# The re-layout transfers of the kept exponentials move from SyncE's to ScalarE's queue, and the TensorE's background items get new steps

## The reference, cut to what matters

```python
q = _qz_ring(heads + rx_theta)                     # 16 heads of width 8, 4096 tokens an image here
scores = jnp.einsum('bhsd,bhtd->bhst', q, q) / np.sqrt(D)
attn = jax.nn.softmax(scores, axis=-1)
ctx = jnp.einsum('bhst,bhtd->bhsd', attn, q)
```

## Time and profile before

| | us |
|---|---|
| time before, median of 3 runs | 7771.48 (7758.5 to 7775.35) |
| the profiled execution, span | 7878.3 |
| ScalarE busy in it | 6811.0 (86%) |
| TensorE busy in it | 6921.9 (88%) |
| VectorE busy in it | 4954.8 (63%) |
| first and last exponential of the main stage | about 791 and 7635 |

### The profile page before, as it was taken

One profiled execution on the slowest core, in us unless ns is written; L12 is line 12 of the kernel. 1 busy time (PEld: TensorE's weight loads), 2 busy tenths in 40 slices (PEclk: granted clock), 3 DMA queues, 4 the chain that ended last, 5 costly groups with the idle time before them and its releaser, 6 DMA issues. The chain is left out here.

```text
span 7878.3 us, 154169 instructions
## 1 busy us (share of the span) xinstructions
PE 6921.9 (88%) x58691; PEld 1859.1 (24%) x58691; DVE 4954.8 (63%) x12688; ACT 6811.0 (86%) x5455; POOL 1244.3 (16%) x1165
## 2 busy tenths in 40 slices
PE   4555799999999999999999999999999999999987
PEld 1444121111121222222221212222222212222224
DVE  5566555555555777777676767777775545454763
ACT  1222799999999999999999999999999999999971
POOL 1553111111111112111221111121210000000000
PEclk8777899999999999999999999999999999999997
DMA  6776575757566556656564545554643333232338
GB/s 214 208 210 185 125 167 138 171 137 166 141 159 147 147 135 169 154 131 157 124 144 112 138 115 132 120 136 113 145 117 77 98 74 92 69 98 64 99 98 265
DMA packets 1744564, 1080.93 MB, mean 137 GB/s; under 512 B 347914, under 2 KB 1645632, under 8 KB 1742828
## 3 DMA queue, kind: packets, MB, share of 16 engines
q1 hardware_dynamic: 1650972, 767.00, 40.2%
q0 software_dynamic: 92880, 304.42, 13.9%
HBM read 410.43 MB, written 190.83 MB: 76 GB/s over the span
## 5 line engine op out<-in xcount | busy, mean ns | idle before, releaser
L1255 ACT ACTIVATE e<-sc 128x1536 f32<-128x1536 f32 x4192 | 5715.2, 1604 | 193.2 <-PE sc L1157 121.7
L1189 PE MATMUL acc<-e,v_cur 128*9 128x512 f32 x25152 | 3341.7, 599 | 45.5 <-DVE acc_sb L1092 44.4
L1157 PE MATMUL sc<-b_unit,a_cur 32*128 32x512 f16 x14592 | 1916.7, 388 | 358.3 <-ACT e L1255 277.2
L1157 PEld LDWEIGHTS sc<-b_unit,a_cur 32*128 32x128 f16 x14592 | 472.6, 91 | 3826.3 <-ACT e L1255 2890.3
L1151 DVE STREAM_TRANSPOSE e_turned<-e_turned 128x1024 f32<-128x1024 f32 x896 | 1060.7, 1221 | 147.9 <-DMA e_turned<-e_kept 114.8
L1255 ACT ACTIVATE e_kept<-sc 128x1536 f32<-128x1536 f32 x672 | 960.6, 1567 | 63.0 <-PE sc L1157 32.1
L757 POOL DMA_INDIRECT room<-taps,idx_st x432 | 520.4, 1205 | 2109.0 <-ACT e L1255 890.2
L757 POOL DMA_INDIRECT corners<-taps,idx_st x441 | 435.1, 987 | 2052.3 <-ACT e L1255 1563.5
L1189 PE MATMUL acc<-e_kept,v_cur 128*9 128x512 f32 x4032 | 715.0, 611 | 0.0
L1189 PEld LDWEIGHTS acc<-e,v_cur 128*9 128x9 f32 x25152 | 394.3, 88 | 797.9 <-issue 730.8
L1180 PE MATMUL acc<-e_turned,v_cur 128*9 128x256 f32 x7168 | 472.2, 381 | 0.0
(11 more groups left out here) (421 smaller groups left out, 5222.5 us busy)
## 6 DMA issues: line engine op xcount, KB each, us to landing
e_turned<-e_kept SPq DMA_DIRECT2D x3584, 128.0 KB
taps<-conv_vals SPq DMA_DIRECT2D x256, 288.0 KB
taps<-cf_tapped SPq DMA_DIRECT2D x128, 288.0 KB
ew<-in_ew SPq DMA_DIRECT2D x12, 1024.0 KB, 7.8
ew<-in_ew SPq DMA_DIRECT2D x48, 256.0 KB, 6.8
x_ch<-in_x SPq DMA_DIRECT2D x4, 2048.0 KB, 12.6
qn<-q SPq DMA_DIRECT2D x64, 128.0 KB
ctx<-ctx_t SPq DMA_DIRECT2D x128, 64.0 KB
```

The costliest lines, as they stand in the source:

```text
L1157: last = self.nc.tensor.matmul(self.sc[k % self.SC][:, i, :], self.a[rows, t * P:(t + 1) * P], self.bst[u % 2][rows, :], start=True, stop= ...
L1189: last = self.nc.tensor.matmul(self.acc[32 * h:32 * h + self.E1, :], self.v[:, t, h, :], src, start=(i == 0), stop=(i == self.UNIT - 1))
L1255: self.nc.scalar.activation(out, self.sc[k % self.SC][:], ACT.Exp, scale=1.0 / HD ** 0.5).then_inc(self.exp_done, 1)
```

## The change

Three things. First, the source layout: `e_kept` was indexed slab, then column; now it is column block (4), slab (9), 128 columns, so that what one transfer takes from a partition is one piece of 4 KB and not 8 pieces of 512 bytes. The exponential writes it in a pattern of 3 x 4 x 128, and the scores are read in the same order. Second, the 16 transfers of a half are issued by ScalarE, two behind each of eight exponentials, from the one that follows the third kept one. The waits of L1134 and L1136 stand in ScalarE's queue ahead of the first two. SyncE's queue loses them all. Third, `PLACES` has new steps for all kinds but "last"; order and number of the items are the same.

```diff
-    SHUFFLES = 16
+    SHUFFLES, ISSUES = 16, 8
...
-        self.kept = sb("e_kept", [P, 9, CHUNK])
+        self.kept = sb("e_kept", [P, 9 * CHUNK])
+        self.kept_by = self.kept[:].rearrange("p (c s x) -> p s c x", c=4, s=9)
...
-    def shuffle_sp(self, sp, qd, u, half):
...
-                sp.dma_start(dst.rearrange("p (s x) -> p s x", x=P), src).then_inc(self.shuffled[half], 16)
+    def shuffle_act(self, act, qd, u, half, part):
+
+
+        if part == 0:
+            used = self.plan.last_turned(u, half) + 1 if u else self.plan.last_turned(UNITS - 1, half) + 1 - UNITS * self.UNIT
+            act.wait_ge(self.pv_done, qd * (UNITS * self.UNIT) + (self.PV_START + used))
+            act.sem_inc(self.r.passed, 1)
+            act.wait_ge(self.exp_done, qd * self.QUAD_STEPS + (self.plan.halves[u, half] + 3 + self.SC))
+        for at in range(part * self.SHUFFLES // self.ISSUES, (part + 1) * self.SHUFFLES // self.ISSUES):
+            a, c = divmod(at, 4)
+            src = self.kept[32 * a:32 * a + 32, c * 9 * P:c * 9 * P + self.KEPT * P]
+            act.dma_start(self.turned[32 * c:32 * c + 32, a, half, :], src).then_inc(self.shuffled[half], 16)
...
-                    src = self.kept[:, self.WIDE * plan.kept_step[k][2] + at, :]
+                    src = self.kept_by[:, self.WIDE * plan.kept_step[k][2] + at]
...
+        issues = {k0 + 3 + i: (u, half, i) for (u, half), k0 in plan.halves.items() for i in range(self.ISSUES)}
...
-            self.nc.scalar.activation(out, self.sc[k % self.SC][:], ACT.Exp,
-                                      scale=1.0 / HD ** 0.5).then_inc(self.exp_done, 1)
+            self.nc.scalar.activation(out, src, ACT.Exp, scale=1.0 / HD ** 0.5).then_inc(self.exp_done, 1)
+            if k in issues:
+                self.shuffle_act(act, qd, *issues[k])
...
         "conv ffn": (
-            5, 25, 28, 46, 49, 51, 53, 55, 66, 72, 77, 78, 82, 85, 106, 109, 121, 124, 128, 129, 132, 144, 149, 154, 155, 156, 159,
+            5, 24, 26, 46, 48, 51, 53, 55, 65, 71, 74, 76, 77, 84, 106, 108, 121, 123, 126, 128, 130, 140, 146, 149, 151, 152,
...
-                    at.shuffle_sp(sp, qd, 0, 0)
...
-                at.shuffle_sp(sp, qd, 2 * p, 1)
```

More of the change, by code:

```diff
@@ L1251, in quad_act @@
                     act.wait_ge(self.shuffled[1 - half], qd * (self.BLOCKS * 16 * self.SHUFFLES) + (16 + 16 * self.SHUFFLES * blocks))
-                out = self.kept[:, self.WIDE * i:self.WIDE * (i + 1), :]
+                out, src = self.kept_by[:, self.WIDE * i:self.WIDE * (i + 1)], self.sc[k % self.SC][:].rearrange("p s (c x) -> p s c x", c=4)
             else:
-                out = self.e[plan.slot[k]][:]
-            self.nc.scalar.activation(out, self.sc[k % self.SC][:], ACT.Exp,
-                                      scale=1.0 / HD ** 0.5).then_inc(self.exp_done, 1)
+                out, src = self.e[plan.slot[k]][:], self.sc[k % self.SC][:]
+            self.nc.scalar.activation(out, src, ACT.Exp, scale=1.0 / HD ** 0.5).then_inc(self.exp_done, 1)
+            if k in issues:
+                self.shuffle_act(act, qd, *issues[k])
 def within(*buffers):
@@ L1604, in stage_main @@
         "conv first": (
[L1605 to L1606 removed]
+            2, 5, 7, 10, 12, 30, 31, 46, 48, 51, 53, 55, 62, 64, 69, 74, 88, 90, 94, 96, 98, 106, 110, 121, 125, 130, 158, 160,
+            164, 166, 168, 170, 172, 175, 178, 181, 195, 199, 204, 233, 235, 239, 241, 243, 245, 247, 250, 252, 256, 270, 294,
+            296,
         ),
         "conv": (
[L1609 to L1610 removed]
+            3, 5, 7, 9, 11, 19, 23, 46, 50, 55, 83, 85, 89, 91, 93, 101, 105, 121, 125, 130, 158, 160, 164, 166, 168, 170, 172,
+            175, 178, 181, 195, 199, 204, 233, 235, 239, 241, 243, 245, 247, 250, 252, 256, 270, 294, 296,
         ),
         "conv ffn taps": (
[3 rows of a table removed]
[4 rows of a table added]
         ),
         "conv ffn": (
[L1618 to L1620 removed]
+            5, 24, 26, 46, 48, 51, 53, 55, 65, 71, 74, 76, 77, 84, 106, 108, 121, 123, 126, 128, 130, 140, 146, 149, 151, 152,
+            159, 181, 183, 195, 198, 200, 202, 204, 215, 221, 223, 226, 227, 234, 256, 258, 260, 270, 272, 293, 295, 297, 299,
+            301, 303, 304,
         ),
         "ffn six": (
[3 rows of a table removed]
[3 rows of a table added]
         ),
         "ffn choice": (
[3 rows of a table removed]
[3 rows of a table added]
         ),
         "ffn": (
[3 rows of a table removed]
[3 rows of a table added]
         ),
         "last": (
[4 rows of a table removed]
[4 rows of a table added]
         ),
@@ L1701, in conv_quad @@
                     at.store_ctx(sp, qd, 2 * p - 1)
-                if not (first and p == 0):
-                    at.shuffle_sp(sp, qd, 2 * p, 0)
                 conv.load_sp(sp, n + LEAD + 1)
@@ L1728, in conv_quad @@
                 if p < QPAIRS - 1:
-                    at.shuffle_sp(sp, qd, 2 * p + 1, 0)
                     if first and p == 0:
@@ L1772, in last_quad @@
             store_gate(FFN_PAIRS)
-            for half in range(2):
-                at.shuffle_sp(sp, qd, 0, half)
             for u in range(1, UNITS):
```

9 lines of the change are left out of this document (removed), and 33 rows, old and new, of the table PLACES.

## The result

The changed kernel takes 8095.8 us, median of 4 runs (8090.4 to 8114.3), against 7772.9 (7758.5 to 7775.4): a ratio of 1.0424, 95% interval 1.0408 to 1.0440. That is 323 us slower where 40 us faster was forecast, and outside the range.

The account below looks back on a forecast made before the run. ScalarE and TensorE were taken as both close to full in the main stage. Terms -20 + 0 + 5 + 0 - 45 + 20 = -40 us against the median 7771.5 gave 7731, written 7732; range 7650 to 7970, the forecast's own 7705 to 7755.

Parts of the forecast that it names:

- the issuing on ScalarE's queue: Two transfers issued behind an exponential take 0.84 us of a 1.35 us step, so they cost 0.
- Rival A: Issues on ScalarE's queue don't fit in a step: 80 to 310 us lost, 7810 to 8045, likeliest 7930; chance 0.18.
- The new steps: TensorE's moved items: -45 us from half its waits for VectorE, +20 us from steps with too much in them.
- rival B: TensorE's pile-ups win, as at step 172 of quads 1 to 3: +40 us, sum +25, 7797 us; chance 0.09.
- SyncE's queue: Loses 2400 us of issuing, its other transfers come earlier, but ScalarE doesn't wait for what is behind them: 0.
- The waits for the transfers: ScalarE's 19.9 us of waits for the kept exponentials' transfers should go: -20 us, bounds 0 and -35.
- VectorE's waits: VectorE's 114.8 us of waits for the same transfers should fall well under that.
- The wait ahead of the first pair: The wait for TensorE now stands before ScalarE's next exponential: +5 us, at most +33, at least 0.
- The layout: The 3 x 4 x 128 pattern that ScalarE writes and TensorE reads keeps runs of 512 bytes: 0.

Follow-up runs that it names:

- Experiment 3: The kernel before with the new layout of e_kept alone, transfers still issued by SyncE: 7745.0 us, ratio 0.9971.
- experiments 6 and 7: 64 columns a transfer, not 1024, with new layout and old steps: issued on ScalarE's queue (6) 7869.7 us, on SyncE's (7) 7697.7 us.
- experiment 1: The kernel before with the new PLACES steps alone, transfers and layout as before: 7896.1 us, ratio 1.0164.
- experiment 4: The changed kernel with the transfers put back on SyncE's queue, new layout and new steps kept: 7876.7 us, ratio 1.0137.
- experiment 10: Experiment 4 with three tap items of quads 0 to 3 moved from steps 175, 178, 181 to 181, 184, 187: 7837.4 us, ratio 1.0096.
- experiment 2: The changed kernel with the old PLACES steps, new layout and transfers on ScalarE's queue kept: 8022.0 us, ratio 1.0324.
- experiment 8: New layout and old steps, SyncE issuing eight transfers of a half and ScalarE eight, one behind each of eight exponentials: 7686.7 us, ratio 0.9898.

## Why the prediction was wrong

**The step that failed is the issuing on ScalarE's queue**, costed at 0 from the one-piece rows: 0.33 + 0.43 and two gaps, 0.84 us a step. Measured are 0.51 and 0.61, 1.16 us for a pair. Those rows are of other transfers (128 partitions, between SBUF and DRAM); the row of this very transfer, minimum 585 and median 622 ns, was in the same group and was set aside by the guess that its eight pieces made it long. Experiment 3 shows a minimum of 507 and a median of 592 with one piece. Rival A had the mechanism, and its condition: from 0.55 us an issue on. It priced the queue at 80 to 310 us; it is 277 with the old steps and 219 in the changed kernel. The whole came out above A's 8045, as A had kept the gain from the new steps. Its detail was off: I put most on the first pair, which loses no more than the others. A pair of 1.16 us and 0.17 us up to the next exponential just fit into a step of 1.34, so each step is paid for by whatever is late in it. The rule that I leaned on, the Trainium skill's "Advanced Engine Details and Errata", Sequencer Loop, agrees with the trace, where transfers are issued beside a running exponential (6035.08 and 6035.10). It says only that the work overlaps. It doesn't say that it fits.

**The tail.** A median was set against the room in a step. Nine issues in a hundred are above 0.82 us, and with 1792 steps without slack each of them is paid. The 105 of the 277 us that go with the bytes (experiments 6 and 7) fit this: the medians are alike, and the issue time beyond 0.62 us differs by 109 us.

**The new steps**, -45 + 20, measured +127 to +132 on SyncE's queue, +74 on ScalarE's, +95 with the queues shared. The waits for VectorE did go: 37.8 + 35.2 + 29.6 = 102.6 us of before are 18.0 in after (17.5 at the staging, 0.5 at the finish of a unit, no row for the gate). The new steps alone gave 41 of this: in experiment 1 the gate has 23.7 us, the staging 38.1, and the finish no row for `acc_sb`. So the 45 us of waits that I had counted on did go, and the time rose all the same, by 127: TensorE is busy for 1174 of 1243 us in quads 1 to 3, and what it doesn't wait at one place it is late at another. That was rival B's argument. B was right too at step 172 (experiment 4): 3.9 us forecast, 3.86 measured, a stall of 2 us forecast, 2.15 measured. It was short at 40 us for two reasons. It missed the wait for a transfer: I moved items against VectorE and never against SyncE's queue, which feeds the taps (34 to 39 us, experiment 10). And it took pile-ups for single steps; this second reason is argued and not shown.

**SyncE's queue**, costed at 0: that held for ScalarE, but the 58 us by which the parts exceed the whole probably come partly from it. In the changed kernel SyncE is free, and no wait for columns shows, where experiment 4 has 33.0 us. **The waits for the transfers**, -20: measured 32.6 to 5.0 us, so -28. Right, and small beside the rest. **VectorE's waits** for the transfers did not fall (129.2 to 131.7). With the old steps they do, from 116.6 in experiment 3 to 76.5 in 2; the new steps take that back. **The wait ahead of the first pair**, +5: no run shows a cost; in experiment 8 it stands there, and the burst runs at full pace. **The layout**, 0: it gives 24.5 us. Its part in the forecast was only to make the issues short, which it hardly did.

So of my cases A and B both happened, and I had treated them as excluding each other. Each alone would have left the forecast (experiments 2 and 4).

What stays open: which step costs what of the remaining 53 to 58 us in quads 0 to 3 and of the 40 in the others (no run separates them), how the layout saves 24.5 us, and whether 32 partitions or both ends in SBUF make the issue 0.51 us long. Fewer, larger transfers were not tried.

## What to carry to other kernels

A transfer moved into a computing engine's queue is priced by the issue time of that same transfer, from its own row, as a sum per step against the time of a step, with room for its slowest tenth; a fit to within 0.2 us was no fit here. When a queue is too long, share it before moving it: one issue a step on ScalarE with eight fewer on SyncE won 53 to 58 us, while two a step on ScalarE cost 277. Before an item is moved earlier on TensorE, look up everything that it waits for, the transfers in another engine's queue first; and waits that vanish on a full engine are a gain only if the engine that it serves waits less.

## What was not expected of the hardware

- No row of before had an issue behind an exponential. An issue right behind another on ScalarE's queue took 612 ns, a lone one 515, both with 4 KB and with 256 bytes in each of 32 partitions. On SyncE's queue the median was 592 and 591.
- Long issues come with the bytes on ScalarE's queue: with small transfers nine in a hundred are over 0.62 us, with full ones over 0.82, and the longest took 2.8 (experiment 2).
- Sharing eight and eight gained 53 to 58 us though no byte less was moved. The Trainium skill, "DMA: Bandwidth & Descriptors", Issuing engines are not separate DMA queues, says that issuing from several engines saves only the time of initiating on the sequencer, "which is usually small relative to the DMA itself". The first half fits the gain. The second is no reason to leave the initiating out of a sum: 3584 x 0.6 us are 2150 us of a queue, in a main stage of 6803. How long the transfers themselves take no row here shows.
